# Moving two of eight probability scalings from GpSimd to ScalarE, with a fifth buffer and transposes one slot later, in a differential attention kernel on one core

## What is computed

```python
dots = einsum('bhqd,bhkd->bhqk', q, k)            # 16 heads of 32, T = 1024
attn_w = softmax(dots)                             # over the keys
attn_w = attn_w.reshape(B, H, 2, T, T)
attn_w = attn_w[:, :, 0] - lam * attn_w[:, :, 1]   # 8 pairs of heads
attn = einsum('bhqk,bhkd->bhqd', attn_w, v)        # then an RMS norm, gamma, @ Wout
```

## Time and profile before

| what | us |
|---|---|
| median of 3 runs | 1417.99 (1416.45 to 1418.41) |
| the profiled execution, its own time | 1416.29 |
| its span, first to last instruction | 1414.2 |
| busy in the span: PE, DVE, ACT, POOL | 1238.8, 1186.1, 1046.3, 1094.1 |
| mean granted TensorE clock (1 is full) | 0.966 |

### The profile page before, as it was taken

The page is one execution under the profiler, slowest core; times in us unless marked ns, Lnnn a source line. Parts: engine busy times, 40 slices in busy tenths (PEclk is TensorE's granted clock), DMA queues, the critical chain, the costliest instruction groups (busy, mean ns, idle before and its releaser), DMA issues. The chain is left out here.

```text
span 1414.2 us, 24279 instructions
## 1 busy us (share of the span) xinstructions
PE 1238.8 (88%) x8370; PEld 749.8 (53%) x8370; DVE 1186.1 (84%) x1969; ACT 1046.3 (74%) x1935; POOL 1094.1 (77%) x778
## 2 busy tenths in 40 slices
PE   2789999999999999999999999988851599999997
PEld 1444444444444444444444444444431588888897
DVE  5899999999999999999999999998757366767665
ACT  2798888888888888888888888888633365556553
POOL 3899999999999999999999999999933443434330
PEclk9799999999999999999999999999975799999999
DMA  4232111121111112111111211110021776868670
GB/s 111 71 89 61 38 44 51 36 66 41 51 51 31 51 42 61 40 51 51 31 53 44 65 31 51 30 31 1 1 50 24 136 126 109 146 106 141 106 130 10
DMA packets 184600, 86.87 MB, mean 61 GB/s; under 512 B 150176, under 2 KB 166048, under 8 KB 184480
## 3 DMA queue, kind: packets, MB, share of 16 engines
q1 hardware_dynamic: 184480, 85.33, 28.7%
HBM read 7.68 MB, written 2.10 MB: 7 GB/s over the span
## 5 line engine op out<-in xcount | busy, mean ns | idle before, releaser
L1233 DVE TENSOR_REDUCE negmax<-score_ps 128x1 f32<-128x1024 f32 x512 | 614.3, 1215 | 58.4 <-PE score_ps L601 56.4
L917 ACT ACTIVATE prob<-score_ps,negmax 128x1024 f32<-128x1024 f32 x512 | 569.5, 1115 | 102.8 <-DVE negmax L1233 101.2
L482 POOL TENSOR_TENSOR prob<-prob 128x1024 f32<-128x1024 f32 x256 | 603.4, 2357 | 21.4
L601 PE MATMUL score_ps<-ka,qa 128*128 128x512 f16 x1024 | 308.9, 384 | 41.9 <-ACT prob L917 28.4
L624 PE MATMUL trans_ps<-ident,prob 128*128 128x128 f32 x2048 | 283.1, 277 | 34.7 <-POOL prob L482 31.6
L624 PEld LDWEIGHTS trans_ps<-ident,prob 128*128 128x128 f32 x2048 | 232.9, 141 | 119.3 <-POOL prob L482 72.5
L480 POOL TENSOR_SCALAR prob<-prob,ccol 128x1024 f32<-128x1024 f32 x256 | 287.1, 1121 | 6.7 <-DVE ccol L1246 6.7
L630 PE MATMUL attn_ps<-probT,v_sb 128*64 128x512 f32 x1024 | 276.8, 620 | 1.1 <-DVE probT L326 1.1
L549 POOL TENSOR_TENSOR xs<-xnT,rw_all 128x2048 f32<-128x2048 f32 x32 | 115.5, 3609 | 168.9 <-DVE prob L1367 162.1
L846 ACT ACTIVATE probT<-trans_ps 128x512 f32<-128x512 f32 x256 | 153.8, 601 | 39.7 <-PE trans_ps L624 37.1
L326 DVE COPY probT<-trans_ps 128x512 f32<-128x512 f32 x256 | 174.1, 680 | 5.5 <-PE trans_ps L624 5.5
(11 more groups left out here) (194 smaller groups left out, 1283.4 us busy)
## 6 DMA issues: line engine op xcount, KB each, us to landing
qa<-split SPq DMA_DIRECT2D x256, 64.0 KB, 2.0
ka<-split SPq DMA_DIRECT2D x256, 64.0 KB, 2.0
xg<-xnT SPq DMA_DIRECT2D x16, 512.0 KB, 3.0
resid<-in_L_attn_x SPq DMA_DIRECT2D x4, 512.0 KB, 5.7
wg<-in_L_attn_Wkv SPq DMA_DIRECT2D x32, 64.0 KB, 2.0
out<-yo SPq DMA_DIRECT2D x32, 64.0 KB, 2.4
wg<-in_L_attn_Wq SPq DMA_DIRECT2D x16, 64.0 KB, 1.9
xsT<-prob SPq DMA_TRANSPOSE x64, 4.5
```

Of the source, the lines that this page charges most:

```text
L482: pool.tensor_tensor(prob1[:, u, :], prob1[:, u, :], prob2[:, u, :], ALU.add).then_inc(mix_ok, 1)
L601: mm = pe.matmul(score_ps[:, sub, kh * HALF:(kh + 1) * HALF], qa[:, par, head * 2 + sub, q0:q0 + P], ka[:, par, head * 2 + sub, kh * HALF: ...
L917: act.activation(prob2[:, s % 4, :] if sub else prob1[:, s % 4, :], score_ps[:, sub, :], ACT.Exp, bias=negmax[:, s % 2, sub:sub + 1], accu ...
L1233: dve.tensor_reduce(negmax[:, s % 2, sub:sub + 1], score_ps[:, sub, :], AX.X, ALU.max, negate=True).then_inc(max_ok, 1)
```

## The change

Units at places 2 and 6 of eight (n % 8 in ACT_SCALES) have their prob2 scaled by ScalarE, as an activation Copy with the pointer ccol as its scale, issued right after E1 of the next unit's slot: in slots of place 3 (ahead of the attnT copy) and of place 7. GpSimd then waits for scaled_A and makes the addition alone. An instruction of GpSimd that only counted a semaphore (mix_seen) is gone.

prob1 and ccol get five buffers, T comes four slots behind its unit and V twelve; rows, cols, project, attnT, stat, root and norm follow one slot later each (now places 4, 1, 2, 3, 5, 6 and 0), the addition to resid at place 3, and the v projections move from place 4 to place 3. k and q fills stay at places 5 and 7. attnT now shares the memory of attn_nT and so waits for project (out_ok) of the half before; yo of part 2 lies in the fifth buffer of prob1.

```diff
-TRANS_LAG = 3
+PROBS = 5
+TRANS_LAG = PROBS - 1
-PV_LAG = 11
+PV_LAG = TRANS_LAG + 8
-PROJ_SLOTS = {4: ("v1", 0), 5: ("k0", 1), 7: ("k1", 1), 12: ("v0", 1), 13: ("q0", 2), 15: ("q1", 2)}
+PROJ_SLOTS = {3: ("v1", 0), 5: ("k0", 1), 7: ("k1", 1), 11: ("v0", 1), 13: ("q0", 2), 15: ("q1", 2)}
+ACT_SCALES = (2, 6)
-FIRST_SLOTS = {0: ("ln", 0), 1: ("ln", 1), 2: ("ln", 2), 3: ("q0", 1), 6: ("q1", 1), 8: ("ln", 3), 9: ("ln", 4), 10: ("ln", 5)}
+FIRST_SLOTS = {0: ("ln", 0), 1: ("ln", 1), 2: ("ln", 2), 4: ("q0", 1), 6: ("q1", 1), 8: ("ln", 3), 9: ("ln", 4), 10: ("ln", 5)}
...
-        prob1 = sb("prob1", [P, 4, T])
+        prob1 = sb("prob1", [P, PROBS, T])
-        ccol = sb("ccol", [P, 4])
-        attnT = sb("attnT", [P, HALF])
+        ccol = sb("ccol", [P, PROBS])
+        attnT = attn_nT.rearrange("p t q -> p (t q)")
-        yo = sb("yo", [P, 2, C])
+        yo = prob1[:, 4, 0:2 * C].rearrange("p (r c) -> p r c", r=2)
+        def act_scaled(units):
+            return sum(n % 8 in ACT_SCALES for n in range(units))
...
-                pool.wait_ge(c_ok, n + 1)
-                pool.sem_inc(mix_seen, 1)
-                pool.tensor_scalar(prob2[:, u, :], prob2[:, u, :], ccol[:, u:u + 1], 1.0, ALU.mult, ALU.mult).then_inc(scaled_P, 1)
-                pool.wait_ge(scaled_P, n + 1)
-                pool.tensor_tensor(prob1[:, u, :], prob1[:, u, :], prob2[:, u, :], ALU.add).then_inc(mix_ok, 1)
+                if n % 8 in ACT_SCALES:
+                    pool.wait_ge(scaled_A, act_scaled(n + 1))
+                else:
+                    pool.wait_ge(c_ok, n + 1)
+                    pool.tensor_scalar(prob2[:, n % 4, :], prob2[:, n % 4, :], ccol[:, u:u + 1], 1.0, ALU.mult, ALU.mult).then_inc(scaled_P, 1)
+                    pool.wait_ge(scaled_P, n + 1 - act_scaled(n + 1))
+                pool.tensor_tensor(prob1[:, n % PROBS, :], prob1[:, n % PROBS, :], prob2[:, n % 4, :], ALU.add).then_inc(mix_ok, 1)
...
-                        if sub == 0 and not (first and s < 4):
-                            act.wait_ge(trans_ok, 2 * (n - 3))
+                        if sub == 0 and n >= PROBS:
+                            act.wait_ge(trans_ok, 2 * (n + 1 - PROBS))
...
+                    if n >= 1 and s <= SLOTS and (n - 1) % 8 in ACT_SCALES:
+                        act.wait_ge(c_ok, n)
+                        r = (n - 1) % PROBS
+                        act.activation(prob2[:, (n - 1) % 4, :], prob2[:, (n - 1) % 4, :], ACT.Copy, scale=ccol[:, r:r + 1]).then_inc(scaled_A, 1)
...
-                            act.wait_ge(rows_ok, 4 * it + half)
+                            act.wait_ge(out_ok, 4 * it + half)
```

More of the change, by code:

```diff
@@ L179, in block_kernel @@
         causal = sb("causal", [P, P], BF16)
-        prob1 = sb("prob1", [P, 4, T])
+        prob1 = sb("prob1", [P, PROBS, T])
         prob2 = sb("prob2", [P, 4, T])
         x2c = prob2.rearrange("p b (t c) -> p (b t) c", c=C)
-        x2sq = prob1
-        xs_split = prob1[:, :, :].bitcast(F16).rearrange("p (r n) (e c) -> p r n e c", r=2, c=C)
+        x2sq = prob1[:, 0:4, :]
+        xs_split = prob1[:, 0:4, :].bitcast(F16).rearrange("p (r n) (e c) -> p r n e c", r=2, c=C)
         x2n = xnT.rearrange("p (t c) -> p t c", c=C)
@@ L269, in block_kernel @@
         low_ok = {"q": sem("q_low_ok"), "k": sem("k_low_ok")}
-        v_ok, scaled_P, mix_seen = sem("v_ok"), sem("scaled_P"), sem("mix_seen")
+        v_ok, scaled_P, scaled_A = sem("v_ok"), sem("scaled_P"), sem("scaled_A")
         score_ok, max_ok, exp_ok, rec_ok, c_ok, mix_ok = (sem(n) for n in ("score_ok", "max_ok", "exp_ok", "rec_ok", "c_ok", "mix_ok"))
@@ L508, in units @@
                 for u in range(8):
-                    mix(8 * h + u, u % 4)
+                    mix(8 * h + u, (8 * h + u) % PROBS)
                     if tail and u == ROOT_AFTER:
@@ L623, in slots @@
                                 k0 = (kb * 4 + t) * P
-                                mm = pe.transpose(trans_ps[:, kb, t * P:(t + 1) * P], prob1[:, u % 4, k0:k0 + P], ident[:, :])
+                                mm = pe.transpose(trans_ps[:, kb, t * P:(t + 1) * P], prob1[:, (n - TRANS_LAG) % PROBS, k0:k0 + P], ident[:, :])
                             mm.then_inc(trans_ok, 1)
@@ L912, in softmax @@
                         act.wait_ge(max_ok, 2 * n + sub + 1)
-                        if sub == 0 and not (first and s < 4):
-                            act.wait_ge(trans_ok, 2 * (n - 3))
-                        if sub == 1 and not (first and s < 4):
+                        if sub == 0 and n >= PROBS:
+                            act.wait_ge(trans_ok, 2 * (n + 1 - PROBS))
+                        if sub == 1 and n >= 4:
                             act.wait_ge(mix_ok, n - 3)
-                        act.activation(prob2[:, s % 4, :] if sub else prob1[:, s % 4, :], score_ps[:, sub, :], ACT.Exp,
+                        act.activation(prob2[:, n % 4, :] if sub else prob1[:, n % PROBS, :], score_ps[:, sub, :], ACT.Exp,
                                        bias=negmax[:, s % 2, sub:sub + 1],
@@ L1240, in slots @@
                     if last_unit:
-                        half, u = ((s - 1) // 8) % 4, (s - 1) % 8
+                        half, u, c = ((s - 1) // 8) % 4, (s - 1) % 8, (n - 1) % PROBS
                         dve.wait_ge(exp_ok, 2 * n)
@@ L1245, in slots @@
                         dve.wait_ge(rec_ok, n)
-                        dve.tensor_scalar(ccol[:, (s - 1) % 4:(s - 1) % 4 + 1], recip2[:, r:r + 1], sums[:, half, 0, u:u + 1],
+                        dve.tensor_scalar(ccol[:, c:c + 1], recip2[:, r:r + 1], sums[:, half, 0, u:u + 1],
                                           lam[:, 5:6], ALU.mult, ALU.mult).then_inc(c_ok, 1)
```

## The result

The changed kernel takes 1489.52 us (1487.56 to 1490.49, 4 runs) against 1417.22 (1416.27 to 1418.41, 4 runs) for the one before: a ratio of 1.0509, 95% interval 1.0497 to 1.0522. It is 72 us slower. 1410 was forecast, with a range up to 1421.

A forecast was written before the change was run, and what follows sets the result against it. GpSimd (POOL), never idle, was taken as the bound. Gains of 6.2 us in the loop, 1.3 in the drain and 0.5 in the first slots sum to 8.0, giving 1410.0 us as median, range 1402 to 1421.

The forecast's parts named there:

- Nothing of its list changes: VectorE's instructions in eight slots were said to stay the same, with stat costing 0.66 us.
- the lags: Later stages and the fifth buffer were said to cost nothing while margins stand, stat moving from place 4 to 5.
- my rivals: Three other outcomes: an even exchange (20%, mean 1418), ScalarE slowing the loop (13%), the slots loosening (7%, 1386 us).
- the slower one: Rival at ScalarE's two scalings: spaced from 1.20 us on, slower by more than 0.2%; 1427 us at 1.30; chance 13%.
- POOL's saving: GpSimd in eight slots: two scalings less save 2.34 us, from 30.76 to 28.42, worth 72 us if nothing else bound.
- VectorE alone would stop at 28.6 us: VectorE's own work in eight slots sums to 28.6 us, which alone caps the gain at 66 us.
- The price of the scaling: On ScalarE, each scaling was taken to cost 1.02 us of spacing, with 0.95 and 1.10 as ends.
- The chain: Closed chain of deciding starts through all engines over eight slots, holding both scalings: 30.53 us against 30.73, gaining 6.2 us.
- The drain: After the last unit: last mix starts 3.6 us or so after its factor instead of 4.96, a gain of 1.3.
- The sum: Gains of 6.2, 1.3 and 0.5 make 8.0 us: 1408.3 like for like, 1410.0 as median.
- the first slots: Start of the loop, without V: a gain between 0 and 2 us, taken as 0.5.
- What would show it: List of signs: right if eight slots take 30.5 us; wrong if under 30.3 or over 30.8, among others.

The follow-up runs named there:

- experiments 1 and 3: Changed kernel with stat's tensor_scalar moved to ScalarE (1410.21 us), or replaced on VectorE by a copying tensor_reduce, GpSimd multiplying by the constant (1411.1 us).
- experiment 1: Changed kernel with the tiny tensor_scalar of the RMS term done by ScalarE ahead of its logarithm: 1410.21 us, ratio 0.9949 to the kernel before.
- the lags alone: Changed kernel with ACT_SCALES empty, so five buffers and later stages but all scalings on GpSimd: 1420.44 us, ratio 1.0026 to the kernel before.
- the scalings alone: Changed kernel with four buffers and the old lags and fills, units 2 and 6 still scaled by ScalarE: 1416.71 us, ratio 0.9996 to the kernel before.

## Why the prediction was wrong

**The step that failed** is the one on DVE: "Nothing of its list changes", with stat at 0.66, and its repetition under the lags, "Stat moves from place 4 to 5 and gives DVE cover there". I took the 0.66 of stat, in which the tensor_scalar has 0.07, from one half and carried it to another place, as if an instruction on VectorE cost the same wherever GpSimd is. It does not: this one takes 0.16 us where it ran free and what is left of GpSimd's instruction where it is held; here it cost VectorE 2.05 us in place of the 0.07. The change moves the instruction by a slot and shifts GpSimd's work against VectorE's at the same time; I checked each moved instruction against the semaphores alone, and there is none between these two. None of my rivals had this place either; the slower one put its price on ScalarE, where nothing was amiss.

**The trace of before showed it.** A look at the line by itself gives the spread, and the two cases behind it (the second stretch is from the timeline around 143 us):

```profile
L1273 DVE TENSOR_SCALAR tl<-sums x32: 157/160/1858, 113.2 to 1041.5; 128x8 f32<-128x8 f32 x32
```
```profile
112.16 2.36 POOL L482 TENSOR_TENSOR prob<-prob 128x1024 f32<-128x1024 f32 x1
...
113.16 1.39 DVE L1273 TENSOR_SCALAR tl<-sums 128x8 f32<-128x8 f32 x1
```
```profile
142.94 1.12 POOL L480 TENSOR_SCALAR prob<-prob,ccol 128x1024 f32<-128x1024 f32 x1
...
143.50 0.59 DVE L1273 TENSOR_SCALAR tl<-sums 128x8 f32<-128x8 f32 x1
```

1.39 us, ended 0.03 after the addition's end at 114.52; 0.59, ended 0.03 after the scaling's at 144.06. A median of 160 and a maximum of 1858 ns for 8 elements is the sign. From the third half to the last step it ran free, and always at the same point: it began 0.02 to 0.06 us after the recorded start of a scaling. Why it was not held there, no run shows; the recorded starts may be off by as much. The 1858 ns belong to the drain, against GpSimd's additions for the second block.

**What of the rest held.** Measured on experiments 1 and 3, which are the changed kernel without the hold:

- *POOL's saving*: right. POOL is busy 27.5 of 30.55 us, or 90.7 of 100 (93 forecast), and waits for ScalarE's tile, for root and for norm, as said; TensorE never waits for line 490. That VectorE alone would stop at 28.6 us was not reached in any run (29.90 at best).
- *The price of the scaling*: taken as 1.02 of spacing, measured 1.04, and 1.137 long. Here the estimate from the Trainium skill, page "ScalarE: Activation LUTs", section "What ACT_TABLE_LOAD costs" (1.13 and 1.04), was the better one.
- *The chain*: 30.53 forecast, 30.54 measured without the instruction and 30.62 with it in a form that is not held (the chain had its 0.07). The wait of VectorE at place 4 was forecast at 0.8 and is 0.80. At place 0 it is 0.19 before M1 and 0.26 before "low", less than the 0.6 given.
- *The drain*: the last mix forecast 3.6 us after its factor. In experiment 1 it starts at 1014.87, the factor being ready at 1011.32: 3.55.
- *The sum*: 1410.0 forecast, 1410.21 and 1411.1 measured, and that the first two agree is in part luck. By the profiled executions the kernel of experiment 1 gains 4.7 us (1414.2 to 1409.5 of span), not 8.0. The factor of unit 23 comes 2.6 us later than before, where 0.5 of gain was forecast for the first slots. From there to the last unit's factor it gains 6.1 (6.2 forecast, but as 31 equal periods: the kernel before runs at 30.73 only from about 175 us on, at 29.5 to 29.8 before that, and 2.4 of the 6.1 come in the last step). The drain gives 1.2 (1.3 forecast). The medians are 7.0 apart, for that profiled execution was the slowest of its four.
- *What was missing*: one term. It is 1.98 of hold and a mean of 0.69 of lower clock in each period (33.28 against 32.59 at full clock), 27 x 2.67 = 72 us, and the rest of 1489.52 - 1410.21 = 79.3 in the first half and in the last step.
- *The lags*: free by semaphores as I said, and alone within 3 us; but they put the instruction inside an addition.

The range failed because it held the uncertainty of the terms that I had, and none for a term that I had not. "What would show it" named eight slots over 30.8 as a sign of being wrong, and that is what the profile shows.

What is left open: where the 3 us of the lags alone (1.0026) come from. Their period is that of the kernel before; the profiled executions are 1.8 us apart, and nearly all of it comes after the last unit's factor. Nor is it known what sets the pace of the scalings alone, 30.80 us: GpSimd waits for ScalarE's tile there (54.6 us in 700) and no transpose waits for GpSimd. And it is open in which halves the clock falls.

## What to carry to other kernels

- One engine can hold another without a semaphore. Before moving an instruction of VectorE, look at the minimum, median and maximum of its line: where the maximum is far over the median, compare its ends with the ends of GpSimd's instructions. An instruction that must stand among GpSimd's long ones is better put in a form that is never held (here a reduction, or another engine) even where it happens to be free now.
- A bound that is removed takes away the slack that hid other costs. Ask of each part what slack pays for it, and whether another part removes that slack.
- Work given to an engine goes where the engine idles, not where it is ready to be issued: the same two scalings left the kernel 7 us under the one before when they stood behind the exponential, and 25 us ahead of it (both with the RMS term on ScalarE).

## What was not expected of the hardware

- A tensor_scalar of VectorE over 128 x 8 float32, memory to memory, was held by GpSimd's tensor_tensor and tensor_scalar alike until 0.02 to 0.04 us after their end, up to 2.14 us; a tensor_reduce of the same shape (0.15), a tensor_scalar of one element (0.27) and copies from PSUM (0.68) were never held.
- The hold has a second price. In three halves of four, about a us after an idle time of 2.49 us, the granted clock of TensorE fell (0.51 from 526 to 529 us), and the period was 0.8 to 1.1 us longer than one with the same hold at full clock (33.4 to 33.7 against 32.6). In the fourth it stayed at 1.00 after the same idle time (2.48).
